# First attention of a four-stage transformer kernel: key-half maxima by a difference and a Relu, weight tiles tested in one operation

## The reference, cut to what matters

```python
q = (x @ Wq.T).reshape(b, t, N_HEADS, HEAD_DIM)
kv_latent = x @ Wkv_down.T
k = (kv_latent @ Wk_up.T).reshape(b, t, N_HEADS, HEAD_DIM)
v = (kv_latent @ Wv_up.T).reshape(b, t, N_HEADS, HEAD_DIM)
scores = jnp.einsum('bqhd,bkhd->bhqk', q, k) * HEAD_DIM ** (-0.5)
attn = jax.nn.softmax(scores, axis=-1)
out = jnp.einsum('bhqk,bkhd->bqhd', attn, v)
return out.reshape(b, t, N_HEADS * HEAD_DIM) @ Wo.T
```

## Time and profile before

| | us |
|---|---|
| median of 3 runs | 2384.83 |
| lowest, highest of them | 2381.47, 2396.0 |
| the profiled execution | 2388.71 |
| its span, first to last instruction | 2386.9 |
| mean granted TensorE clock | 0.99 |

### The profile page before, as it was taken

One profiled execution on the slowest core, in us unless ns is written; L12 is line 12 of the kernel. 1 busy time (PEld: TensorE's weight loads), 2 busy tenths in 40 slices (PEclk: granted clock), 3 DMA queues, 4 the chain that ended last, 5 costly groups with the idle time before them and its releaser, 6 DMA issues.

```text
span 2386.9 us, 38698 instructions
## 1 busy us (share of the span) xinstructions
PE 2302.6 (96%) x14913; PEld 1425.2 (60%) x14913; DVE 1532.2 (64%) x2110; ACT 1346.0 (56%) x1793; POOL 1045.0 (44%) x674
## 2 busy tenths in 40 slices
PE   7989999999998999999999999999999999999999
PEld 4445555555444888888888887444444444444588
DVE  7887887877874224322421323879889889889364
ACT  3555555555444444444444443578778778777743
POOL 1657777766666436746646555030000000000354
PEclk8999999999999999999999999999999999999999
DMA  2121321321212455555555556433333333322232
GB/s 62 62 70 54 98 81 55 98 80 54 72 43 72 167 169 180 184 189 181 179 196 177 184 193 181 118 96 83 93 75 68 93 73 70 93 83 49 71 113 80
DMA packets 156836, 259.02 MB, mean 109 GB/s; under 512 B 37004, under 2 KB 97292, under 8 KB 156300
## 3 DMA queue, kind: packets, MB, share of 16 engines
q1 hardware_dynamic: 156652, 256.53, 35.7%
HBM read 206.52 MB, written 60.68 MB: 112 GB/s over the span
## 4 chain that ended last, share of the span: by engine, by line
PE 61%; ACT 2%; DMA 2%; DVE 1%; issue 1%; SPq 1%; POOL 0%; POOLq 0%; ACTq 0%
PE m_R L129 45%; PE m_O L129 10%; PE m_X L129 4%; DMA m_K<-bounce_k 1%; ACT m_P L1766 1%; PE m_X L226 1%; SPq L1624 1%; DVE m_mraw L1918 1%; ACT m_OS L1773 0%; DVE m_ln_x L205 0%; PE m_X L2132 0%; PE m_R L226 0%; DMA bounce_k<-m_comp 0%; DMA inverses<-m_rinv 0%; ACT m_comp L1786 0%
## 5 line engine op out<-in xcount | busy, mean ns | idle before, releaser
L1918 DVE TENSOR_REDUCE m_mraw<-m_R 128x2 f32<-128x1024 f32 x512 | 622.0, 1220 | 68.0 <-PE m_R L129 56.7
L1766 ACT ACTIVATE m_P<-m_R 128x1024 f32<-128x1024 f32 x512 | 523.6, 1025 | 152.1 <-PE m_R L129 151.8
L755 DVE TENSOR_REDUCE a_mraw<-a_X 128x1 f32<-128x512 f32 x496 | 317.9, 682 | 93.3 <-PE a_X L129 92.5
L614 ACT ACTIVATE a_P<-a_S 128x1024 f32<-128x1024 f32 x256 | 248.6, 1022 | 203.4 <-PE a_S L129 203.3
L129 PE MATMUL m_O<-m_P,m_V 128*17 128x256 f32 x4096 | 329.4, 393 | 4.5 <-ACT m_P L1766 2.5
L129 PE MATMUL a_O<-a_P,a_V 128*64 128x512 f32 x1024 | 252.3, 615 | 7.3 <-ACT a_ON L622 7.3
L2023 POOL TENSOR_TENSOR m_act0l<-m_xf,m_act0h 128x512 fp32r<-128x512 f32 x128 | 164.8, 1290 | 209.9 <-ACT m_xf L1828 111.7
L926 POOL TENSOR_TENSOR a_accp<-a_accp,a_P 128x1024 f32<-128x1024 f32 x96 | 249.5, 2599 | 13.7 <-ACT a_P L614 4.5
L129 PE MATMUL m_R<-m_act0h,wt 128*128 128x512 f32 x640 | 251.5, 393 | 0.0
L129 PE MATMUL m_R<-m_act0l,wt 128*128 128x512 f32 x640 | 250.4, 391 | 0.0
L129 PE MATMUL m_R<-m_Q,m_K 64*128 64x512 f32 x800 | 200.2, 497 | 2.7 <-DVE m_mraw L1918 2.4
(11 more groups left out here) (265 smaller groups left out, 4068.8 us busy)
## 6 DMA issues: line engine op xcount, KB each, us to landing
wt<-wcopy SPq DMA_DIRECT2D x176, 512.0 KB, 3.4
m_K<-bounce_k SPq DMA_DIRECT2D x96, 128.0 KB, 5.4
m_ln_x<-x SPq DMA_DIRECT2D x23, 512.0 KB, 3.9
a_tile<-in_L_ffn_tiles SPq DMA_DIRECT2D x22, 512.0 KB, 4.5
wcopy<-in_L_ffn_tiles SPq DMA_DIRECT2D x22, 512.0 KB, 5.2
x<-xres SPq DMA_DIRECT2D x78, 128.0 KB, 2.9
m_Q<-bounce_q SPq DMA_DIRECT2D x150, 64.0 KB, 2.3
xres<-x SPq DMA_DIRECT2D x64, 128.0 KB, 2.8
```

The costliest lines, as they stand in the source:

```text
L614: act.eng.activation(P[n % NP][:, :, :], psS[n % 2][:, :, :], ACT.Exp, scale=SCALE).then_inc(s_exp)
L755: dve.eng.tensor_reduce(mraw[u % 2][:, t, h:h + 1], bank(key), AX.X, ALU.max).then_inc(X.free(key))
L1766: act.eng.activation(P[h % 4][:, :, :], pair(key)[:, :, :], ACT.Exp, scale=SCALE).then_inc(R.free(key))
L1918: dve.eng.tensor_reduce(mraw[u % 2][:, at, :], pair(key)[:, :, :], AX.X, ALU.max).then_inc(R.free(key))
```

## The change

For a query quarter the two halves' largest score is taken from one stream: with a = Q·K[512:] and b = Q·K[:512], max(a, b) = b + Relu(a - b). Once per batch TensorE makes the difference K[512:] - K[:512] (`key_halves`, two matmuls with the identity and its negative, a new user of the ring) and VectorE rounds it into `halves` (`keep_halves`). Even steps now multiply Q with `halves`; ScalarE writes their positive part to `excess` in SBUF (`surplus`), in the turn ahead of the exponentials. Odd steps multiply Q with K[:512]; VectorE adds `excess` and takes the maximum in one `tensor_tensor_reduce` per head. `reduce` of even steps is gone from VectorE. Of the 12 early steps the even ones lie in `psS`. A weight tile is tested by one `scalar_tensor_tensor` with `not_equal` and a sum in place of subtraction and reduction; its steps move to j = 2 (load), 3 (round), 1 (compare) for the 22 and j = 2, 3 (cast), 0 (round), 1 for the five, which are now loaded into `tile_hi`; the compare moves behind the rest of VectorE's turn. `spread` and `minus` move into a shared weight buffer.

```diff
+        self.wt_all = sb("wt", [128, 3, 1024], F32R)
+        self.wt = [self.wt_all[:, i, :] for i in range(3)]
...
-    LOWS0, LOWS, LOW_FIRST = 22, 27, 3
+    LOWS0, LOWS, LOW_FIRST = 22, 27, 6
...
+        n, step = divmod(4 * u + j - LOW_FIRST, 4)
+        if not 0 <= n < LOWS:
+            return None
+        return n, (("load", "round", "", "compare") if n < LOWS0 else ("load", "cast", "round", "compare"))[step]
...
+            out += [("halves", halves_at(u, j))] if halves_at(u, j) else []
...
+            def surplus(n, h):
+
+                if early(n):
+                    act.wait_ge(s_early, n // 2 + 1)
+                else:
+                    act.wait_ge(*X.filled(("max", n, h)))
+                if n >= 2:
+                    act.wait_ge(*X.emptied(("max", n - 1, h)))
+                freed = s_excess if early(n) else X.free(("max", n, h))
+                act.eng.activation(excess[:, h, :], max_bank(n, h), ACT.Relu).then_inc(freed)
...
                 if out_at(u, j):
                     out_high(*out_at(u, j))
+                if 2 * (m + AHEAD) < STEPS:
+                    for h in range(NH):
+                        surplus(2 * (m + AHEAD), h)
                 for n in (2 * m, 2 * m + 1):
                     exponent(n)
...
+            def keep_halves(b):
+                key = ("halves", b)
+                dve.wait_ge(*X.filled(key))
+                dve.eng.tensor_copy(halves[b % 2], bank(key).rearrange("p (i n) -> p i n", i=2)).then_inc(X.free(key))
...
+                for h in range(NH):
+                    key = ("max", n, h)
+                    dve.wait_ge(*((s_excess, n - 1 + h + 1) if early(n - 1) else X.emptied(("max", n - 1, h))))
+                    dve.wait_ge(*X.filled(key))
+                    dve.eng.tensor_tensor_reduce(excess[:, h, :], bank(key), excess[:, h, :], 1.0, LOWEST, ALU.add, ALU.max,
+                                                 mraw[u % 2][:, q, h:h + 1]).then_inc(X.free(key))
...
+                    dve.eng.tensor_scalar(mneg[:, :, :], mraw[u % 2][:, :, :].rearrange("p q h -> p h q"), -1.0, None, ALU.mult).then_inc(s_max)
...
-                    dve.eng.tensor_tensor(low[:, :], tile[:, :], f32(tile_hi[:, :]), ALU.subtract).then_inc(s_tile_lo)
-                elif step == "reduce":
-                    dve.wait_ge(s_tile_lo, n + 1)
-                    dve.eng.tensor_reduce(lows[:, n:n + 1], low[:, :], AX.X, ALU.max, apply_absolute_value=True).then_inc(s_low)
+                    dve.eng.scalar_tensor_tensor(f32(tile_hi[:, :]), tile[:, :], 0.0, f32(tile_hi[:, :]), ALU.add, ALU.not_equal,
+                                                 accum_out=lows[:, n:n + 1]).then_inc(s_low)
...
-                if ahead < STEPS:
-                    reduce(ahead)
                 if m:
                     for n in (2 * m - 2, 2 * m - 1):
                         add(n)
-                if tile_at(u, j):
-                    tile_low(*tile_at(u, j))
                 if ahead < STEPS:
                     reduce(ahead + 1)
...
+                if tile_at(u, j):
+                    tile_low(*tile_at(u, j))
                 if norm_at(u, j):
                     norm_step(*norm_at(u, j))
...
+            def key_halves(b):
+                key = ("halves", b)
+                pe.wait_free(X, key)
+                pe.wait_ge(s_identr, 2)
+                for half in range(2):
+                    pe.wait_ge(s_lathi, 2 * b + half + 1)
+                products(pe, bank(key), [(identr[:, :], Kh[b % 2][:, 512:T]), (minus[:, :], Kh[b % 2][:, 0:512])]).then_inc(X.full(key))
...
+                    x = Kh[b % 2][rows, 0:512] if n % 2 else halves[b % 2][rows, :, :]
+                    ins = mm(pe, max_bank(n, h), Qh[u % 3][rows, 128 * q:128 * q + 128], x)
```

More of the change, by code:

```diff
@@ L333, in x_order @@
         out = [("turn", 0, i % 2, i // 2) for i in range(4)] + [("latent", 0, half) for half in range(2)]
-        out += [("q", u) for u in range(2)] + [("values", 0)]
+        out += [("q", 0), ("halves", 0), ("q", 1), ("values", 0)]
         for n in range(2 * AHEAD):
-            out += [("max", n, h) for h in range(NH)] if early_banks(n) is None else []
+            out += [("max", n, h) for h in range(NH)] if n % 2 else []
             out += [("differ", 0, 1), ("differ", 0, 0), ("rows", 0)] if n == NT - 1 else []
@@ L353, in x_order, with early @@
         return out + [("out", *pending), ("sums", NU - 1)] + [("out", b, t) for b, t in TAIL]
-    def early_banks(n):
-        return n % 3 - 1 if n < 2 * AHEAD and n % 3 else None
+    def early(n):
+        return n < 2 * AHEAD and n % 2 == 0
     with ExitStack() as ctx:
@@ L438, in max_bank @@
         def max_bank(n, h):
-            if early_banks(n) is not None:
-                return psS[early_banks(n)][:, h, :]
-            return bank(("max", n, h))
+            return psS[n // 2 % 2][:, h, :] if early(n) else bank(("max", n, h))
         def p_freed_by_adds(n):
@@ L747, in reduce @@
                     dve.wait_ge(s_max, u - 1)
-                if early_banks(n) is not None:
-                    dve.wait_ge(s_early, 2 * (n // 3) + n % 3)
-                    dve.eng.tensor_reduce(mraw[u % 2][:, t, :], psS[early_banks(n)][:, :, :], AX.X, ALU.max).then_inc(s_taken)
-                else:
-                    for h in range(NH):
-                        key = ("max", n, h)
-                        dve.wait_ge(*X.filled(key))
-                        dve.eng.tensor_reduce(mraw[u % 2][:, t, h:h + 1], bank(key), AX.X, ALU.max).then_inc(X.free(key))
@@ L764, in reduce @@
+                if q == NT // 2 - 1:
+                    for k in range(n, n - NT, -2):
+                        for h in range(NH):
+                            dve.wait_ge(*X.emptied(("max", k, h)))
                     if u:
                         dve.wait_ge(*X.filled(("rows", u - 1)))
-                    dve.eng.tensor_reduce(mneg[:, :, :], halves, AX.X, ALU.max, negate=True).then_inc(s_max)
+                    dve.eng.tensor_scalar(mneg[:, :, :], mraw[u % 2][:, :, :].rearrange("p q h -> p h q"), -1.0, None, ALU.mult).then_inc(s_max)
@@ L795, in tile_low @@
             def tile_low(n, step):
-                low = tile if n < LOWS0 else f32(itile[:, :])
                 if step == "cast":
@@ L839, in vector @@
                 latent_low(0, half)
-            for u in range(2):
-                query_low(u)
+            query_low(0)
+            keep_halves(0)
+            query_low(1)
             def way_low(i):
@@ L847, in way_low @@
                                       f32(wo[0][rows, g, :]), ALU.subtract).then_inc(X.free(("way", i)))
-            for n in range(2 * AHEAD):
+            for n in range(1, 2 * AHEAD, 2):
                 reduce(n)
@@ L1098, in tensor @@
             pe.wait_ge(s_wlo, 5)
-            for u in range(2):
-                query(u)
+            query(0)
+            key_halves(0)
+            query(1)
             pe.wait_ge(s_identr, 1)
```

90 lines of the change are left out of this document (43 added, 47 removed).

## The result

Median after: 2363.02 us over 6 runs (2359.25 to 2371.68), before 2384.31 over 6 runs. The ratio is 0.9909, 95% interval 0.9884 to 0.9933: faster by 0.9%, just under the 1% that the chances were drawn at. The forecast was 2359; by these medians the gain is 21.3 us where the forecast had 26. The profiled execution after took 2364.05 us with a span of 2362.0, before 2388.71 and 2386.9; the sum of the prediction, on this basis, said 2362.5.

A forecast was written before the change was run, and what follows sets the result against it. TensorE, 96% busy, was taken to lose time waiting for VectorE's reductions. Terms -38 - 3.3 - 3.5 + 6.2 + 7 + 2.5 + 1.9 + 1 = -26.2 us gave 2362.5 profiled, 2359 from the median; own range 2348 to 2371, with rivals 2338 to 2392.

The forecast's parts named there:

- The waits for VectorE: First attention: TensorE's waits for banks that VectorE's reductions had not emptied go, -38 us, bounds -29 and -46.
- before the first turn: The 12 early steps on VectorE get shorter, first scores at 37.7 us: -3.5 us, bounds 0 and -6.
- clock: Two of four slow-clock windows, those following a wait for a reduction, go: -3.3 us, bounds 0 and -6.7.
- out_high: At j = 1 from unit 6, `keep_out` and `out_high` delay the Relu, bank 0.24 us late, 26 times: +6.2 us.
- unit 5: Unit 5 of a batch: ScalarE's scaling of x makes waits 9.3 instead of 7.3 us, +2, and delays next-turn Relus, +5.
- the tile's rounding and the residual: Rounding at j = 3 ends late, +1.5, with other side work another +1; reductions still late here and there, +1 us.
- The combined reduction: VectorE's tensor_tensor_reduce for the maxima takes 0.8 us, bounds 0.68 and 1.37 us.
- rival 2: Combined reduction on VectorE runs at half rate, 1.37 us; half of the 38 us stays: 2378 us; chance 0.13.
- The tile test: VectorE's one-operation test takes 2.2 us, bounds 1.2 and 3.4; behind the reductions at j = 1, it delays no bank.
- ScalarE's cushion: In an ordinary turn the Relu ends 0.3 us before it would delay the bank that TensorE wants next.
- take VectorE's place: Rival: late Relus on ScalarE cost TensorE 0.45 us in each of 122 turns: slower, 2414 us; chance 0.10.
- The tile test as a brake: Rival: tile test near 3 us on VectorE holds up norm steps and GpSimd's adds, some 8 us: 2367; chance 0.12.

The follow-up runs named there:

- Run 9: Kernel after with the tile tests of before: subtraction at j = 1, reduction at j = 2, both ahead of the maxima; 2365.49 us.
- Run 4: Kernel after with each tensor_tensor_reduce as an addition and a reduction, the bank freed after the second; 2436.3 us.
- run 11: Kernel after with the negation `mneg` written by a tensor_reduce with negate instead of tensor_scalar; 2363.41 us.
- run 2: Kernel before with the whole tile part of the change (one operation, new place), the maxima as before; 2376.45 us.
- run 3: Kernel after with the tile test as two operations again, both in turn j = 1 at the new place; 2380.68 us.
- run 10: Kernel after with the two-operation tile test at the new place in j = 1, and `mneg` by tensor_reduce with negate; 2375.82 us.
- run 5: Kernel after with `out_high` moved behind the two Relus of its turn; 2361.1 us.
- run 8: Kernel after with the first Relu of every turn done twice, the bank freed by the second; 2406.04 us.
- run 12: Kernel after with both `out_high` behind the Relus and `mneg` by tensor_reduce with negate; 2353.42 us.
- run 6: Kernel after with the scaling of normalised x on VectorE in place of ScalarE; 2369.72 us.

## Why the prediction was right, point by point

- **The waits for VectorE, -38:** held. The shown ones fall by 29.2 us (30.9 to 1.7). From the stage's end the whole term can be worked out: the last exponentials start at 724.53 in place of 749.09, -24.6. Take out the other terms as they measured (before the first turn -1.8, clock -1.7, out_high +6.5, unit 5 +6.9) and `key_halves` (+1.9): -36.4, or down to -40 if the tile's rounding and the residual cost the 3.5 that I gave them; `key_halves` and these two stand at their forecast, they were not measured by themselves. So the term is a remainder, not a measurement. The picture behind it, a small gap in the ordinary turn, was not the main thing: taken from the first scores of each turn, 72 of 127 turns of after are within 0.2 us of before, and eleven turns (units 2 to 5 at j = 1, and seven in units 23 to 28) hold 18 us. In nearly all of them a tile operation of 1.2 to 3.4 us stood on VectorE. Run 9 keeps those operations and still has nearly all of the gain. My reading, which no run isolates: with half as many banks to empty, VectorE may be late for a moment without TensorE waiting.
- **The combined reduction, 0.8 us:** 688 + 83 ns = 0.77 by the rows, in 256 places, and 0.61 from bank to bank. Run 4 shows that this was the condition of the gain, and there my price failed: rival 2 at 2378 counted VectorE's busy time ("the tiles' relief; half of the 38 us stays"), where at 1.37 us a bank the time was 2436. What counts is how long the chain through one of three banks and `excess` takes.
- **The tile test, 2.2 us:** 1.42 in after, but there the negation ahead of it has mostly waited for GpSimd already: with a negation that does not wait (run 11), or with the test in the kernel before (run 2), the same instruction takes 2.40 and 2.33 us, and negation and test together take 2.7 in after. Its least is 1210 ns with 76 for the reading of the sum. The rule that I had from the Trainium skill (Vector Engine (DVE) Microarchitecture Reference, Points that are easy to get wrong), half rate with two non-bf16 sources in SBUF, is not borne out: 1024 elements take as long as in the one-source L807. "So it delays no bank" held for one operation; run 3 shows that it holds by 1 to 2 us only.
- **The negation:** not in my sum at all. It changed from a reduction, 0.17 us in all 32 places of before, to a tensor_scalar and takes 1.3 us on average, 35 us in all. In the kernel after, this fell into VectorE's slack (run 11: no change); with more behind it, or a little later, it does not (run 10 against run 3; unit 6 of run 5). The copy of `halves`, for me "a turn ahead of its reader", is that only in the program: in unit 6 of after it ends at 176.40 and the product that reads it starts at 176.49.
- **The clock, -3.3:** half. One window at 0.66 (3.4 us at 1.2 GHz), one at 0.50 and 1.8 us more at 0.82: 10.2 us against 13.6 before, -1.7 us. The two low stretches begin at waits for the Relu in units 21 and 29, behind `scale_act`, as I had said. Over all six executions of after the mean clock is 0.992, the same as before, so no gain from the clock is shown beyond the profiled pair.
- **Before the first turn, -3.5:** -1.8. The first scores start at 39.36, not 37.7. The pairs follow each other by 1.45 to 1.76 us, where I had 1.6, and the hole for differences and rows is 3 us, not 2. Part of both is TensorE's clock, which I had not priced here: granted 0.61 from 31 to 37 us, which is mostly the lower level (before 0.50). In runs 9 and 11 the first scores start at 39.16 and 38.75, so some of the term varies from run to run.
- **ScalarE's cushion, 0.3 us:** 0.3 at j = 2 and 3 (run 8). `out_high` at j = 1, 0.24 us late: 0.26 in the 18 plain turns (runs 5 and 12 against after); it is 25 times, not 26, for the last unit has no Relu, so 6.5 us. Unit 5: I had 9.3 + 5 = 14.3 us of waits for the Relu; the row says 14.2 in nine places. Four behind the first scaling take 1.9 to 3.6 us (10.1 in all), three behind the second 1.23 each (3.7), so the sum fits better than its parts. The two of the first batch:

```profile
146.23 0.50 PE L130 MATMUL a_X<-a_Kh,a_Qh 64*128 64x512 f32 x2 [2.76 <-ACT a_excess L597]
...
152.21 0.51 PE L130 MATMUL a_X<-a_Kh,a_Qh 64*128 64x512 f32 x2 [1.23 <-ACT a_excess L597]
```

- **Rivals.** ScalarE does not take VectorE's place in ordinary turns, though some 0.45 us more in every turn would have made the change worth nothing (an estimate from run 8's turns: 0.15 us beyond the cushion in 60 turns at j = 2 and 3, the full 0.45 in 25 at j = 1, is 20 us). The tile test as a brake was real only in the form of run 3.
- **Shares.** The maxima alone are worth 18 us (run 9), the tile part 8 us alone (run 2) and 2.5 us on top of the maxima, less than the two can be told apart. My sum took them together and did not say this.
- **Luck.** The terms for the clock and for the start missed the same way, by 3.3 us together. That the profiled pair still comes within 1.6 us of the sum is because others erred the other way; the remainder for the waits and the 3.5 us for rounding and residual cannot be told apart. And the main term rests on a middle between two bounds 17 us apart.

## What to carry to other kernels

Price an added operation by how much longer it makes the chain through the scarce buffer, not by the engine's share of busy time: 0.7 us more per bank in the timeline cost 73 us here while VectorE was 76% busy in the stage. Before work is moved to the end of a turn, add up everything that stands there in that one turn, small instructions included, for the same two tile operations cost 2.5 us in two turns ahead of the maxima and 17.7 us together at the end of one. And where a reordering gives less than it should, compare turn by turn: it gave its 0.26 us in every plain turn, and lost 0.96 us in three turns where a copy stood behind the shifted negation.

## What the runs showed of the hardware

A tensor_scalar on 128x8 fp32 numbers in SBUF took 0.17 us at 33.08 us of after, when GpSimd was idle, and up to 2.44 us beside GpSimd. Each of the 31 others of after ended within 0.03 us of the end of a GpSimd operation; as above in run 3, 106.31 + 2.16 = 108.47 beside 106.07 + 2.38 = 108.45. The same negation as a tensor_reduce took 160 to 164 ns in all 31 places of run 12, with a GpSimd operation under way in each:

```profile
L785 DVE TENSOR_REDUCE a_mneg<-a_mraw x31: 160/161/164, 48.9 to 690.8; 128x8 fp32r<-128x8 f32 x31
```

The combined reduction, one source in PSUM, never waits so (674 to 693 ns). The Trainium skill (SBUF — State Buffer, SBUF: two separate sides) describes it: VectorE and GpSimd share one pair of ports to SBUF, taken whole by whoever starts first, by VectorE for a two-port mode or, against a GpSimd operation that reads SBUF, two SBUF inputs. The traces agree in each case above. The scaling of x as a tensor_scalar in run 6 is another such case: 0.40 us in the ten pieces that meet no GpSimd operation, against 0.59 on ScalarE, and 0.66 to 2.57 us in the 18 that end 0.15 us behind one.
